# Keys and values from high and low float32r parts, with five reorderings, in a fused cross-attention and mixture-of-experts kernel

## The reference, cut to what matters

```
xn = layernorm(x)
q  = ln(xn @ Wq + bq) per head                    # 16 heads of 32
kv = ctx[:, :-16] @ (Wk | Wv) + (bk | bv)         # 240 keys, 256 -> 1024 columns
k  = ln(kv[..., :32]);  v = kv[..., 32:]          # 64 columns of kv per head
kd, vd from ctx[:, -16:] @ Wkv_dca                # 16 more keys, a softmax of their own
x  = x + (softmax(q k) v + softmax(q kd) vd) @ Wo + bo
g  = top 2 of 6 experts, chosen per batch by softmax(mean(layernorm(x)) @ gate_W)
x  = x + sum_g  w_g * (gelu(xn2 @ W1[g] + b1[g]) @ W2[g] + b2[g])
```

## Time and profile before

| | us |
|---|---|
| median of 3 runs | 1132.83 (1128.11 to 1137.46) |
| the profiled execution | 1133.56 |
| its span, first to last instruction | 1131.7 |
| mean granted TensorE clock | 0.930 |
| attention, by the first instruction of the second phase on VectorE | up to about 780 |
| one full attention step | about 41.8 |

### The profile page before, as it was taken

One profiled execution on the slowest core, in us unless ns is written; L12 is line 12 of the kernel. 1 busy time (PEld: TensorE's weight loads), 2 busy tenths in 40 slices (PEclk: granted clock), 3 DMA queues, 4 the chain that ended last, 5 costly groups with the idle time before them and its releaser, 6 DMA issues. The chain is left out here.

```text
span 1131.7 us, 17393 instructions
## 1 busy us (share of the span) xinstructions
PE 968.7 (86%) x5020; PEld 649.3 (57%) x5020; DVE 797.6 (70%) x1706; ACT 638.8 (56%) x1658; POOL 294.9 (26%) x203
## 2 busy tenths in 40 slices
PE   0756899999999999999999998664599999999998
PEld 0323545545555545555555555332588888888887
DVE  2736778787787787788788777334877777768774
ACT  0223887787888788778778778665322313122131
POOL 0474315315415415424414513000000000000000
PEclk9978899899999899999999999767699999999999
DMA  7015624634634634733634543676011111111110
GB/s 260 28 31 129 147 72 125 152 85 124 151 89 119 157 85 117 178 79 110 171 81 112 151 95 84 145 253 224 2 55 56 56 56 38 55 56 56 56 37 38
DMA packets 56413, 116.41 MB, mean 103 GB/s; under 512 B 13944, under 2 KB 22392, under 8 KB 56120
## 3 DMA queue, kind: packets, MB, share of 16 engines
q1 hardware_dynamic: 53760, 115.16, 37.0%
q10 hardware_dynamic: 2616, 0.79, 0.3%
HBM read 47.24 MB, written 17.30 MB: 57 GB/s over the span
## 5 line engine op out<-in xcount | busy, mean ns | idle before, releaser
L471 POOL TENSOR_TENSOR vs<-vs,neg_half 128x16 f32<-128x16 f32 x66 | 196.1, 2980 | 367.3 <-DVE vs L920 367.3
L798 ACT ACTIVATE sc<-sc,nm 128x240 f32<-128x240 f32 x512 | 222.9, 441 | 66.0 <-DVE ed L968 65.5
L963 DVE TENSOR_REDUCE pm<-sc 128x64 f32<-128x1024 f32 x128 | 156.2, 1221 | 38.2 <-PE sc L625 34.7
L578 PE MATMUL ring<-wq,xT 128*128 128x512 f32 x256 | 144.6, 718 | 21.2 <-ACT xT L766 16.1
L1388 ACT ACTIVATE hb<-hb 128x352 f32<-128x352 f32 x64 | 31.8, 497 | 227.8 <-DVE hb L1444 227.8
L625 PE MATMUL sc<-KS,QS 96*128 96x256 f32 x512 | 107.7, 335 | 44.3 <-ACT sc L798 39.4
L807 ACT ACTIVATE pt<-sc 128x1024 f32<-128x1024 f32 x128 | 124.0, 1024 | 29.4 <-PE sc L646 29.4
L625 PEld LDWEIGHTS sc<-KS,QS 96*128 96x128 f32 x512 | 75.2, 200 | 92.8 <-ACT sc L798 61.3
L591 PE MATMUL ring<-wkv,cT 128*128 128x512 f32 (+1 forms) x256 | 124.4, 611 | 0.9 <-ACT kdT L779 0.9
L678 PE MATMUL ring<-wo,ot 128*128 128x512 f32 x256 | 122.8, 604 | 0.7 <-DVE ot L1010 0.7
L798 ACT ACTIVATION_READ_ACCUMULATOR sc<-sc,nm 128x1 f32 x512 | 109.2, 213 | 0.0
(11 more groups left out here) (137 smaller groups left out, 1632.6 us busy)
## 6 DMA issues: line engine op xcount, KB each, us to landing
KS<-k_hi SPq DMA_DIRECT2D x128, 128.0 KB, 2.3
QS<-q_hi SPq DMA_DIRECT2D x128, 128.0 KB, 3.0
xin<-in_x_dram SPq DMA_DIRECT2D x16, 512.0 KB, 4.0
KS<-k_lo SPq DMA_DIRECT2D x64, 128.0 KB, 2.3
QS<-q_lo SPq DMA_DIRECT2D x64, 128.0 KB, 2.9
xres<-in_x_dram SPq DMA_DIRECT2D x16, 512.0 KB, 3.3
x_scratch<-xres SPq DMA_DIRECT2D x16, 512.0 KB, 4.7
x<-x_scratch SPq DMA_DIRECT2D x16, 512.0 KB, 3.2
```

The costliest lines, as they stand in the source:

```text
L471: pool.tensor_tensor(w, w, neg_half[0:rows, :], ALU.pow).then_inc(rstd, 1)
L578: last = pe.matmul(bank[:, :], xT[:, kc, t * P:(t + 1) * P], wq[:, kc, :], start=(kc == 0), stop=(kc == KC - 1))
L798: last = act.activation(s, s, ACT.Exp, bias=nm[:, t, h:h + 1], accum_out=den[:, t, h:h + 1])
L963: dve.tensor_reduce(pieces, s.rearrange("p h (c n) -> p h c n", n=DCA), AX_X, ALU.max, negate=True).then_inc(g_max, 1)
```

## The change

- k and v products: `wkv` is split once, before the loops, into `wkv_hi` (a ScalarE copy of 128x2048) and `wkv` (a VectorE subtraction); per batch the transposed context is split into `cT` (ScalarE, as before, now float32r) and `cT_lo` (a new VectorE subtraction of 128x512 between the shift rows and `row_norm`). `project_kv` has three float32r matmuls per `cc` where it had one in float32.
- k's low part is taken after group_max 6 and 7 and the first `dca_sums`, not before them.
- `probabilities` 6 and 7 are ahead of q's affine (QT0, QT1) on ScalarE.
- SP loads x ahead of the q_hi rows, and stores the result between the first and second set of q_hi rows.
- Feed-forward: VectorE reads the expert numbers and does bias 0 ahead of the next batch's row statistics, and bias 1 ahead of `row_norm`; TensorE does the first expert's full chunks of output 0 ahead of HT1. Unit names take other PSUM banks by that.

```diff
-        ("wq", [P, KC, D], F32), ("wkv", [P, CC, 2 * D], F32),
+        ("wq", [P, KC, D], F32), ("wkv", [P, CC, 2 * D], F32R),
...
+    wkv_hi = sb("wkv_hi", [P, CC, 2 * D], F32R)
+    cT, cT_lo = sb("cT", [P, CC, TOK], F32R), sb("cT_lo", [P, CC, TOK], F32R)
...
+            if step in STATS:
+                load_x(b + 4)
             if step in KEYED:
                 sp.wait_ge(split, 4 * (b + 1) + 3)
                 stack_rows(QS, 1 - par, q_hi, 0, q_in)
+            if step in WOUT:
+                wait_evac(sp, step, "WO1", b)
+                sp.dma_start(x2_dram[b - 1], xres[:, :, :]).then_inc(x2_st, 16)
+            if step in KEYED:
                 stack_rows(QS, 1 - par, q_hi, 2, q_in)
                 sp.wait_ge(split, 4 * (b + 1) + 4)
                 stack_rows(QS, 1 - par, q_lo, 1, q_in)
-            if step in STATS:
-                load_x(b + 4)
             if step in WOUT:
-                wait_evac(sp, step, "WO1", b)
-                sp.dma_start(x2_dram[b - 1], xres[:, :, :]).then_inc(x2_st, 16)
                 sp.wait_ge(x2_st, 16 * b)
...
                 if step == "p1":
-                    pe.wait_ge(prep, 4)
-            for cc in range(CC):
-                last = pe.matmul(bank[0:ROWS[c], :], cT[:, cc, c * P:c * P + ROWS[c]],
-                                 kv_half(wkv[:, cc, :], half),
-                                 start=(cc == 0), stop=(cc == CC - 1))
+                    pe.wait_ge(wkv_rdy, 2)
+            parts = [(cc, c_part, w_part) for cc in range(CC)
+                     for c_part, w_part in ((cT, wkv_hi), (cT, wkv), (cT_lo, wkv_hi))]
+            for n, (cc, c_part, w_part) in enumerate(parts):
+                last = pe.matmul(bank[0:ROWS[c], :], c_part[:, cc, c * P:c * P + ROWS[c]],
+                                 kv_half(w_part[:, cc, :], half),
+                                 start=(n == 0), stop=(n == len(parts) - 1))
...
+            if step == "p0":
+                act.wait_ge(prep, 4)
+                act.activation(wkv_hi[:, :, :], wkv_raw[:, :, :], ACT.Copy).then_inc(wkv_rdy, 1)
...
             if proj:
-                copy_out(step, b, "CT", cT[:, :, :], CC * TOK)
+                bank = wait_full(act, step, "CT", b)
+                act.activation(cT[:, :, :], bank[:, :].rearrange("p (a n) -> p a n", a=CC), ACT.Copy
+                               ).then_inc(ct_hi, 1)
                 sq_unit(0)
...
+            if attn:
+                probabilities(step, b, 6)
+                probabilities(step, b, 7)
             if proj:
                 wait(act, split, 4 * (b + 1) + 4)
                 affine_out(step, b, "QT0", qf[:, 0:2, :], affine_q)
...
             if keyed:
-                split_k(step, b)
-            if attn:
-                dca_sums(b, 0)
+                split_k_high(step, b)
+            if attn:
                 group_max(b, 6)
                 group_max(b, 7)
+                dca_sums(b, 0)
+            if keyed:
+                split_k_low(b)
+            if attn:
                 dca_sums(b, 1)
...
+            if proj:
+                dve.wait_ge(ct_hi, b + 3)
+                bank = ring[u.bank(step, "CT")]
+                dve.tensor_tensor(cT_lo[:, :, :], bank[:, :].rearrange("p (a n) -> p a n", a=CC),
+                                  cT[:, :, :].bitcast(F32), ALU.subtract).then_inc(taken(step, "CT"), 1)
             if step in NORM:
                 row_norm(b + 3)
...
+                dve.wait_ge(wkv_rdy, 1)
+                dve.tensor_tensor(wkv[:, :, :], wkv_raw[:, :, :], wkv_hi[:, :, :].bitcast(F32),
+                                  ALU.subtract).then_inc(wkv_rdy, 1)
...
-    BODY = ["H0", "H1", "H2", "HT0", "H3", "XT0", "XT1", "HT1", "HR", "OUT0", "GT", "OUT1"]
+    BODY = ["H0", "H1", "H2", "HT0", "H3", "XT0", "XT1", "OUT0", "HT1", "HR", "GT", "OUT1"]
...
             if ffn:
+                output(step, b, ex, 0, FULL_CHUNKS[0])
                 h_transposes(step, b, 1)
                 last_chunks(step, b)
-                output(step, b, ex, 0, FULL_CHUNKS)
+                output(step, b, ex, 0, FULL_CHUNKS[1])
...
+            if ffn:
+                ex = [dve.value_load(idx[par][0:1, e:e + 1], min_val=0, max_val=NE - 1) for e in range(TOP)]
+                bias(0, ex)
             if does_next:
...
             if ffn:
-                ex = [dve.value_load(idx[par][0:1, e:e + 1], min_val=0, max_val=NE - 1) for e in range(TOP)]
-                bias(0, ex)
+                bias(1, ex)
                 if does_next:
                     row_norm()
-                bias(1, ex)
                 bias(2, ex)
```

More of the change, by code:

```diff
@@ L195, in attention_phase @@
         early[n] for n in "wq wkv xin xh xT q1 kb kf qf q_hi q_lo k_hi k_lo".split())
-    cT = sb("cT", [P, CC, TOK])
+    wkv_hi = sb("wkv_hi", [P, CC, 2 * D], F32R)
+    cT, cT_lo = sb("cT", [P, CC, TOK], F32R), sb("cT_lo", [P, CC, TOK], F32R)
     cin = sb("cin", [P, NC, KD])
@@ L213, in attention_phase @@
     QS = [early["QS0"], sb("QS1", [ST, HP, G, S], F32R)]
+    with ExitStack() as short:
+        wkv_raw = short.enter_context(nc.sbuf_tensor("wkv_raw", [P, CC, 2 * D], F32))
     KS = [sb(f"KS{i}", [ST, HP, G, TOK], F32R) for i in range(2)]
@@ L253, in attention_phase @@
     split = sem("split")
+    ct_hi, wkv_rdy = sem("ct_hi"), sem("wkv_rdy")
     ctx_rdy = sem("ctx_rdy")
@@ L362, in _ @@
         sp.dma_start(cin[:, :, :], ctx_t[0]).then_inc(c_ld, 16)
-        sp.dma_start(wkv[:, :, 0:D], Wk.rearrange("(c p) n -> p c n", p=P)).then_inc(wkv_ld, 16)
-        sp.dma_start(wkv[:, :, D:2 * D], Wv.rearrange("(c p) n -> p c n", p=P)).then_inc(wkv_ld, 16)
+        sp.dma_start(wkv_raw[:, :, 0:D], Wk.rearrange("(c p) n -> p c n", p=P)).then_inc(wkv_ld, 16)
+        sp.dma_start(wkv_raw[:, :, D:2 * D], Wv.rearrange("(c p) n -> p c n", p=P)).then_inc(wkv_ld, 16)
         for dst, src in ((bq_b[:, :], bq), (bkv_b[:, 0:D], bk), (bkv_b[:, D:2 * D], bv)):
@@ L883, in body @@
                     affine_out("p1", -2, f"KD{j}", kdT[:, 2 * j:2 * j + 2, :], affine[:, 4:6])
-            if attn:
-                probabilities(step, b, 6)
-                probabilities(step, b, 7)
         walk(act, body)
@@ L896, in _ @@
             (wq_ld, 16, wq[:, :, :].rearrange("p c (h d) -> p (c h) d", d=HD)),
-            (wkv_ld, 32, wkv[:, :, :].rearrange("p c (h w) -> p (c h) w", w=W)[:, :, 0:HD]),
+            (wkv_ld, 32, wkv_raw[:, :, :].rearrange("p c (h w) -> p (c h) w", w=W)[:, :, 0:HD]),
             (b_ld, 48, bq_b[:, :].rearrange("p (h d) -> p h d", d=HD)),
@@ L987, in bias_k, with split_high, split_low @@
                               kv_half(bkv_b[0:ROWS[c], :], 0), ALU.add).then_inc(taken(step, f"K{c}"), 1)
-        def split_parts(m, n, whole, hi, lo, stacked):
+        def split_high(m, whole, hi, stacked):
             wait(dve, stacked, STACKED * m)
             dve.tensor_copy(hi[:, :, :], whole[:, :, :]).then_inc(split, 1)
+        def split_low(m, n, whole, hi, lo):
             dve.wait_ge(split, 4 * m + n + 1)
@@ L997, in split_q, with split_k_high @@
         def split_q(m):
-            split_parts(m, 2, qf, q_hi, q_lo, q_in)
-        def split_k(step, b):
+            split_high(m, qf, q_hi, q_in)
+            split_low(m, 2, qf, q_hi, q_lo)
+        def split_k_high(step, b):
             for name in ("KT0", "KT1"):
@@ L1005, in split_k, with split_k_low @@
             dve.wait_ge(kd_rdy, b + 2)
-            split_parts(b + 1, 0, kf, k_hi, k_lo, k_in)
+            split_high(b + 1, kf, k_hi, k_in)
+        def split_k_low(b):
+            split_low(b + 1, 0, kf, k_hi, k_lo)
         def ctx_out(step, b, g):
@@ L1301, in last_chunks @@
             last.then_inc(full[u.bank(step, "HR")], 1)
-        FULL_CHUNKS = [(e, fc) for e in range(TOP) for fc in range(FC - 1)]
+        FULL_CHUNKS = [[(e, fc) for fc in range(FC - 1)] for e in range(TOP)]
         LAST_CHUNKS = [(e, FC - 1) for e in range(TOP)]
         def output(step, b, ex, t, chunks):
-            if chunks is FULL_CHUNKS:
+            if chunks is FULL_CHUNKS[0]:
                 bank = begin(pe, step, f"OUT{t}", b)
@@ L1321, in output @@
                                      w2[wp][0:rows, bass.ds(ex[e], 1), fc, :].rearrange("p a n -> p (a n)"),
-                                     start=(chunks is FULL_CHUNKS and n == 0 and i == 0),
+                                     start=(chunks is FULL_CHUNKS[0] and n == 0 and i == 0),
                                      stop=(chunks is LAST_CHUNKS and n == TOP - 1 and i == 2),
@@ L1351, in body @@
             if ffn:
-                output(step, b, ex, 1, FULL_CHUNKS)
+                output(step, b, ex, 1, FULL_CHUNKS[0])
+                output(step, b, ex, 1, FULL_CHUNKS[1])
                 wait_evac(pe, step, "HR", b)
```

## The result

| | median us | range, executions |
|---|---|---|
| before | 1132.28 | 1128.11 to 1137.46, 4 |
| after | 1102.29 | 1100.13 to 1106.82, 4 |

The ratio is 0.974, with a 95% interval from 0.9715 to 0.977. The forecast was 1114.0 with a range from 1100 to 1130. The profiled execution of after took 1106.82 us, the longest of its four; its span is 1105.0, against 1131.7 of before. The difference of the spans, 26.7 us, is cut by events that both traces have: scores 6 of three batches, and the first x transposes of the feed-forward phase.

What follows compares the result with a forecast made beforehand. TensorE, busy 86% of the span, was taken as the bound. 1133.6 - 6.6 (full attention steps) - 1 (step "later") + 1.5 (prologue) - 13.5 (feed-forward) = 1114.0 us, range 1100 to 1130.

Steps and rivals of the forecast that it cites:

- rival 1: Attention: scores 0 never wait for q rows, landing at 434.2; 14 x 0.4 more gained, 1108 us; chance 0.22.
- a faster clock: Range's lower end: the clock gaining half a microsecond a step, together with q rows never waited for, giving 1100 us.
- Feed-forward: TensorE's GELU waits before HT0 and HT1 shrink: 0.85 us a step, first step 1.2, last 0.4; 13.5 us less.
- Cover: Feed-forward: VectorE's residual 1 ends within about 0.1 us of output 0's new end, so a step can't gain more.
- Products: Attention: float32r K and V units shorten TensorE's path by 0.87 us per full step (K0 0.33, K1 0.27, V1 0.27).
- Wait of scores 0: Attention: TensorE waits for the last stacked q row, behind x and the store: 0.4 us a step.
- rival 2: Attention: q rows land at 436.4, scores 0 wait 1.3 us; 1127 us, or 1120 with half; chance 0.18.
- The other orders: Attention: moving k's low part and probabilities 6 and 7 gains 0 in full steps; 1 us in step "later".
- -0.47: Net change per full attention step: 0.87 us gained by products less 0.40 waiting for q rows; 6.6 us over 14.
- Clock: Attention: Q0 stays about 5.4 us, taken as 0; bounds 1.8 us less a step if Q0 reached full clock.
- rival 4: Attention: new TensorE pauses spread the lower clock; Q1 wholly at 1.2 GHz costs 3.6 us a step, 1164; chance 0.05.
- Prologue: Before the loops: the `wkv` copy and subtraction delay Q0 and its bias; net +1.5 us, bounds -1 and +4.

Runs made afterwards that it cites:

- bias_only: Kernel before plus only VectorE's new feed-forward order (expert numbers and bias 0 ahead of statistics, bias 1 ahead of `row_norm`): 1119.09 us, ratio 0.9865.
- out_only: Kernel before plus only TensorE's new feed-forward order (first expert's full chunks of output 0 ahead of HT1): 1125.98 us, ratio 0.9927.
- x_first_hold: Kernel after with the store behind all q rows (x still ahead) and GpSimd's residual bias add held until VectorE normalised k: 1096.16 us, ratio 0.966.
- old_products: Kernel after with the float32 k and v products of before, without the low parts they make unnecessary: 1103.42 us, ratio 0.9748.
- x_first: Kernel after with the store moved behind all q rows, x still loaded ahead of them: 1102.95 us, ratio 0.9736.
- x_first_hold_old_orders: `x_first_hold` with k's low part and probabilities 6 and 7 back in their places of before; against before: 1104.24 us, ratio 0.973.
- ffn_only: Kernel before with the new feed-forward phase, attention phase unchanged: 1111.51 us, ratio 0.9814.
- old_sp: Kernel after with SP's order of before (all twelve q rows, then x load, then store): 1104.17 us, ratio 0.9731.

## Why the prediction was right, and where it was off

The direction, the range and the order of the causes held, and the miss has one main cause. By the spans the saving is 7 us larger than forecast, 9 more in feed-forward and 2 less in attention; the other 4.5 of the 12 us are the distance of the profiled execution of after from its median. Since feed-forward takes the same in every profile with its new order, that distance belongs to attention and the prologue, whose gain is then 4.3 to 7.6 us, with 6.1 forecast. That 1102.3 lies in the range is in part luck: the range's lower end stood for rival 1 and a faster clock, of which neither came, and feed-forward filled the place, although the prediction had said that a step there can't gain more.

- **Feed-forward, 13.5 forecast, 22.4 measured.** This is the mis-sized term. The step that failed is "Of 0.68 us before HT0 about 0.1 stays. The 0.27 before HT1 is covered": I took the idle times as the price. They are counted from the modelled end of the last matmul, 0.33 us after its start, while the next one may start 0.16 after it. So each wait costs 0.16 to 0.24 us more than its row says, and of the 0.1 that was to stay nothing did: 1.34 us a step instead of 0.85. `bias_only` and `out_only` show it for each wait by itself. Fourteen steps gained 18.8 us and not 11.9, the first 2.95 and not 1.2, the last and its tail 0.7 and not 0.4.
- **Cover.** The limit I had named there, VectorE's residual 1, did not bind: TensorE's groups follow each other at their own pace in after.
- **Products, 0.87 us a step.** Right in mechanism and nearly in size, 0.78 measured, but only in `x_first_hold`, where nothing else is late. By its pieces V1 gave 0.3 (third column of the table; forecast 0.27), K0 and K1 0.50 in the first two columns together (5.14 + 9.70 against 4.99 + 10.35 us; forecast 0.60). The mark between these two columns can't be compared across the two products: in before, transposed scores 0 are recorded 1.44 us after K0's start (424.06, 425.50), though K0's four records are 0.43 apart.
- **Wait of scores 0, 0.40 forecast, 0.82 measured** (second column, after against `x_first_hold`); rival 2 had 1.3, rival 1 nothing. It used up the whole gain of the products. `old_products` shows it: the same time without the products. By the means of twelve full steps the last q row was issued 8.75 us after x (forecast 8.3) and landed 3.85 later (forecast 2.9, and 4.0 by the middle that I took). The Trainium skill, "DMA: Bandwidth & Descriptors", section "Queues, rings and completion order", has descriptors of one queue consumed in ring order; the trace agrees in direction: behind the two large transfers the q_hi rows land 3.9 us after issue instead of 3.0 and the q_lo rows 3.5 instead of 2.9, not the full 1.1 for each of the two. In `x_first`, behind x alone, it is 3.8 and 3.6, so what the early store cost the q rows was mostly its place among SP's issues.
- **The other orders, 0 in a full step.** Off by 0.2 to 0.3 with cheaper products (`x_first_hold_old_orders`). I had written that the gains need the move of the probabilities, and still put the price at 0. In before it would have bought 0.15 (second column, before against `old_products`).
- **That the attention step came out at -0.44 against -0.47 is luck.** The parts are -0.78 for products, +0.82 for the wait, -0.15 for the probabilities and -0.30 between Q0 and CT. The last part is no effect of the change that these runs can show: with the attention phase of before unchanged, that piece took 4.58 to 5.27 us in four profiles, and 4.97 in after. By the first five columns alone, up to Q0, the step gained 0.22 us.
- **Clock.** No spread of the lower clock, so rival 4 did not come. Q0 stayed near 5 us. The granted clock was 0.50 over the first 2.5 us of the Q0 shown and 1.00 over Q1. To the start of CT it took about 6.2 us in three of thirteen steps of before and in one of after, which is most of the 0.30, and 3.54, at the full clock, in three steps of `ffn_only`. What decides which steps are so was not tried.
- **Prologue, +1.5 forecast, +2.25 measured.** The copy took 1.91 and the subtraction 2.29 us (forecast 2.0 and 2.4), and Q0's bias came at 39.30 (forecast 40.8). The six profiles with float32r products start batch 0's LT at 129.4 us in the mean, the eight with float32 at 125.7, so the products cost some 3 or 4 us there; single profiles of either kind spread over 4 to 7 us, and overlap.
- **Not foreseen.** The collision of VectorE and GpSimd, which decides between `x_first` and `x_first_hold`. The early store avoids it, at the cost of the wait of scores 0. So after, `old_sp` and `x_first` end within 2 us of each other: each pays 0.5 to 0.9 us a step against `x_first_hold`, at another place. For the products to pay, the q rows, x and the normalise of k all had to be in time.

## What to carry to other kernels

Price a TensorE wait by the distance between the starts of the two matmuls around it, less the distance of undisturbed ones, and not by the idle time listed. When work on one engine gets cheaper and the time stays, look for what became late next, and test the saving again with that removed: here the products were worth nothing in two orders of the DMAs and 7.4 us once GpSimd's add was moved as well. Before a difference between two profiles is explained, look at the same stretch in kernels whose code there is the same: here that alone accounted for up to 0.3 us a step. When DMAs are reordered, follow what each landing releases on the other engines too, GpSimd's included.

## What the runs showed of the hardware

- This VectorE multiplication with two operands in SBUF stood still while GpSimd added two SBUF tensors. The second half of k's normalise takes 0.68 us alone and took 2.87 us from 354.9 on in `x_first`, with GpSimd's add from 354.62 to 357.18: it ended 0.6 us after GpSimd. The Trainium skill, "SBUF — State Buffer", section "SBUF: two separate sides", calls the shared port pair an exclusive lock for which the later one waits in full; these rows agree. VectorE's maxima, which read PSUM, took 1.21 to 1.23 us in all traces, the five of before that lie wholly within an add of GpSimd among them.
- 128 KB transfers issued behind 512 KB ones took 0.6 to 0.9 us longer to land (3.0 to 3.9 us and 2.9 to 3.5, before and after).
- Three float32r matmuls of 512 columns take 0.71 us (0.24 each) where one float32 product takes 0.86 (two records, 0.43 apart).
